# Value matmuls of an attention unit in two groups of eight instead of four groups of four

## What is computed

```python
att = jnp.einsum('bhqd,bhkd->bhqk', q, k) * scale
att = jnp.where(causal[None, None], att, -jnp.inf)      # self attention only
y = jnp.einsum('bhqk,bhkd->bhqd', jax.nn.softmax(att, axis=-1), v)
```

## Time and profile before

| what | value |
|---|---|
| median of three runs | 1836.56 us |
| the profiled execution: span from first to last instruction | 1831.7 us |
| TensorE busy | 1634.0 us, 89% |
| VectorE busy | 1353.5 us, 74% |
| ScalarE busy | 1151.3 us, 63% |
| GpSimd busy | 658.3 us, 36% |
| mean granted TensorE clock | 0.957 of full |

### The profile page before, as it was taken

One profiled execution on the slowest core, in us unless ns is written; L12 is line 12 of the kernel. 1 busy time (PEld: TensorE's weight loads), 2 busy tenths in 40 slices (PEclk: granted clock), 3 DMA queues, 4 the chain that ended last, 5 costly groups with the idle time before them and its releaser, 6 DMA issues.

```text
span 1831.7 us, 29160 instructions
## 1 busy us (share of the span) xinstructions
PE 1634.0 (89%) x10051; PEld 735.1 (40%) x10064; DVE 1353.5 (74%) x2549; ACT 1151.3 (63%) x2178; POOL 658.3 (36%) x915
## 2 busy tenths in 40 slices
PE   5897879998999989998999999988999998899677
PEld 1343335433543435433543344433543543333236
DVE  6677677788588777778687777877488687688287
ACT  1474576566755686667765685657655854756497
POOL 3422524550445234641454135622562242310140
PEclk7898989999999999999999999999999998899899
DMA  7333412323243323332242323332332231124123
GB/s 196 101 108 108 121 35 72 99 79 90 63 117 79 93 59 99 88 101 67 67 113 62 91 77 92 86 102 76 82 105 59 54 102 47 44 77 138 46 70 116
DMA packets 106947, 159.49 MB, mean 87 GB/s; under 512 B 20656, under 2 KB 83248, under 8 KB 106800
## 3 DMA queue, kind: packets, MB, share of 16 engines
q1 hardware_dynamic: 101904, 156.43, 30.8%
q10 hardware_dynamic: 4896, 1.18, 0.3%
HBM read 105.00 MB, written 51.38 MB: 85 GB/s over the span
## 4 chain that ended last, share of the span: by engine, by line
PE 54%; DVE 19%; ACT 10%; POOL 7%; issue 4%; DMA 3%; SPq 1%; ACTq 0%; DVEq 0%; POOLq 0%
PE acc L1492 11%; PE st L1478 10%; PE misc L1457 10%; DVE nmax L1255 8%; PE misc L1432 7%; PE misc L1404 4%; PE misc L1519 3%; PE misc L1444 3%; ACT probs L988 3%; ACT tail_h L1058 2%; ACT tail_h L1043 1%; PE misc L1546 1%; PE misc L1533 1%; POOL parts L873 1%; POOL qk L869 1%
## 5 line engine op out<-in xcount | busy, mean ns | idle before, releaser
L1255 DVE TENSOR_REDUCE nmax<-misc 128x1 f32<-128x512 f32 (+2 forms) x1376 | 863.8, 671 | 301.9 <-PE misc L1457 181.4
L988 ACT ACTIVATE probs<-st 128x512 f32<-128x512 f32 (+3 forms) x1536 | 760.4, 551 | 375.2 <-PE st L1478 241.3
L1457 PE MATMUL misc<-stack 96*128 96x512 bf16 (+3 forms) x1536 | 535.1, 364 | 58.2 <-DVE nmax L1255 41.1
L1478 PE MATMUL st<-stack 99*128 99x512 bf16 (+3 forms) x1536 | 539.8, 362 | 37.6 <-ACT probs L988 31.5
L1478 PEld LDWEIGHTS st<-stack 99*128 99x128 bf16 x1536 | 148.7, 98 | 377.8 <-ACT probs L988 222.0
L1457 PEld LDWEIGHTS misc<-stack 96*128 96x128 bf16 x1536 | 151.9, 99 | 199.1 <-DVE nmax L1255 83.1
L1492 PE MATMUL acc<-probs,v_x 128*32 128x512 f32 x1152 | 157.8, 621 | 0.0
L867 POOL TENSOR_TENSOR parts<-qk,zero 128x512 bf16<-128x512 f32 x78 | 81.3, 1043 | 207.6 <-ACT qk L971 207.6
L879 POOL TENSOR_TENSOR nparts<-nmax,zero 128x16 bf16<-128x16 f32 x96 | 21.3, 222 | 273.3 <-DVE nmax L1255 273.3
L1492 PE MATMUL acc<-probs,v_s 128*32 128x512 f32 (+3 forms) x1152 | 113.6, 466 | 0.1
L1481 PE MATMUL st<-mask_st,identb 128*128 128x128 bf16 x512 | 111.1, 220 | 0.0
(11 more groups left out here) (258 smaller groups left out, 2087.2 us busy)
## 6 DMA issues: line engine op xcount, KB each, us to landing
parts_xk<-parts SPq DMA_DIRECT2D x54, 128.0 KB
parts_xq<-parts SPq DMA_DIRECT2D x54, 128.0 KB
stack<-parts_xq SPq DMA_DIRECT2D x36, 192.0 KB, 3.2
stack<-parts_xk SPq DMA_DIRECT2D x36, 192.0 KB, 3.7
parts_sk<-parts SPq DMA_DIRECT2D x48, 128.0 KB
parts_sq<-parts SPq DMA_DIRECT2D x48, 128.0 KB
stack<-parts_sq SPq DMA_DIRECT2D x32, 192.0 KB, 2.9
stack<-parts_sk SPq DMA_DIRECT2D x32, 192.0 KB, 3.4
```

Of the source, the lines that this page charges most:

```text
L988: act.activation(probs[:, j % P_SLOTS, c, T - w:], st_bank(n, 4 * j + c)[:, 0:w], ACT.Exp, scale=SCALE).then_inc(exp_done, 1)
L1255: dve.tensor_reduce(nmax[:, ring, first:first + NT * (len(cs) - 1) + 1:NT], src, AX.X, ALU.max, negate=True).then_inc(misc_free[slot], 1)
L1457: last = pe.matmul(o, stack[0:ROWS, r, 0, c, P * i:P * i + P], stack[0:ROWS, r, 1, c, 0:w], start=True, stop=not causal)
L1478: last = pe.matmul(o[:, 0:w], stack[0:AUG, r, 1, c, P * j:P * j + P], stack[0:AUG, r, 0, c, T - w:T], start=True, stop=not causal)
```

## The change

The four value groups of a unit become two, each for two tile rows (a pair, `PAIRS` = 2): the first stands after the scores (2, 3), the second after the scores (0, 3) of the next unit. `probs` has three slots, taken in turn over all tile rows of all units, and the first exponential of a tile row waits for the pair that holds the tile row three before it. `v_aug` keeps 18 columns a head (`V_STEP`), of which the matmul takes 17 (`VW`); the zeros go, with the three memsets on GpSimd that made them, and VectorE clears `acc` once at the start, since the matmuls now write 17 of every 32 partitions and the heads copy reads all. The code that is not in this core of the diff only adjusts counts (`NMADE`, `AHEAD`, `VD`).

```diff
-ST_BANKS, MISC_BANKS, P_SLOTS, QK_RING = 3, 4, 2, 4
+ST_BANKS, MISC_BANKS, P_SLOTS, QK_RING = 3, 4, 3, 4
+PAIRS = NT // 2
+VW, V_STEP = D + 1, D + 2
...
-            if c == 3 and j:
-                out.append(("values", u, j - 1))
+            if (j, c) == (2, 3):
+                out.append(("values", u, 0))
             if (j, c) == (0, 3) and prev:
-                out += [("values", prev, NT - 1), ("heads_copy", prev)]
+                out += [("values", prev, PAIRS - 1), ("heads_copy", prev)]
...
-    return [("values", u, NT - 1), ("heads_copy", u), ("heads_out", u)]
+    return [("values", u, PAIRS - 1), ("heads_copy", u), ("heads_out", u)]
...
-        v_aug = {p: lb(f"v_{p}", [P, NT, H, 32]) for p in "xsf"}
+        v_aug = {p: lb(f"v_{p}", [P, NT, H, V_STEP]) for p in "xsf"}
...
+        def probs_slot(n, j):
+
+            tile_ = n.times(NT, j).base
+            return tile_ % P_SLOTS, max(0, (tile_ - P_SLOTS) // 2 + 1)
...
                 pool.memset(v[:, :, :, D:D + 1], 1.0).then_inc(consts_made, 1)
-                pool.memset(v[:, :, :, D + 1:], 0.0).then_inc(consts_made, 1)
...
-                if c == 0:
-                    act.wait_ge(values_done, n.times(4, VD - P_SLOTS + j + 1).at())
+                slot, freed = probs_slot(n, j)
+                if c == 0 and freed:
+                    act.wait_ge(values_done, freed)
                 act.wait_ge(st_full, n.times(16, 4 * j + c + 1).at())
-                act.activation(probs[:, j % P_SLOTS, c, T - w:], st_bank(n, 4 * j + c)[:, 0:w], ACT.Exp, scale=SCALE).then_inc(exp_done, 1)
+                act.activation(probs[:, slot, c, T - w:], st_bank(n, 4 * j + c)[:, 0:w], ACT.Exp, scale=SCALE).then_inc(exp_done, 1)
...
             dve.memset(stack[ROWS:AUG, :, 1, :, :].bitcast(F32), two_ones).then_inc(ones_made, 1)
+            dve.memset(acc[:, :], 0.0).then_inc(ones_made, 1)
...
-                j, n, (_, p, g) = s.args[0], s.n, s.unit
-                w = T - P * j if p == "s" else T
-                if j == 0:
+                pair, n, (_, p, g) = s.args[0], s.n, s.unit
+                if pair == 0:
                     pe.wait_ge(v_done[p], s.b.times(2, 2).at())
                     pe.wait_ge(heads_full, n.at(1))
-                pe.wait_ge(exp_done, n.times(16, 4 * j + 4 + ST_BANKS).at())
-                for c in range(HU):
-                    last = pe.matmul(acc[32 * c:32 * c + 32, T - w:T], v_of(s, p)[:, j, HU * g + c, :],
-                                     probs[:, j % P_SLOTS, c, T - w:T], start=j == 0, stop=j == NT - 1)
+                pe.wait_ge(exp_done, n.times(16, 8 * pair + 8 + ST_BANKS).at())
+                for j in (2 * pair, 2 * pair + 1):
+                    w = T - P * j if p == "s" else T
+                    slot, _ = probs_slot(n, j)
+                    for c in range(HU):
+                        last = pe.matmul(acc[32 * c:32 * c + VW, T - w:T], v_of(s, p)[:, j, HU * g + c, 0:VW],
+                                         probs[:, slot, c, T - w:T], start=j == 0, stop=j == NT - 1)
                 last.then_inc(values_done, 1)
```

More of the change, by code:

```diff
@@ L496, in two_layers_kernel @@
         NFIRST = 6
-        NMADE = 13
+        NMADE = 10
         consts_in, consts_made = sem("consts_in"), sem("consts_made")
@@ L525, in two_layers_kernel @@
         zeroed, waited, picked = sem("zeroed"), sem("waited"), sem("picked")
-        AHEAD = [(free, 1) for free in misc_free] + [(exp_done, ST_BANKS), (values_done, P_SLOTS), (heads_full, 1), (negmax_split, 8), (negmax_landed[0], 16),
+        AHEAD = [(free, 1) for free in misc_free] + [(exp_done, ST_BANKS), (heads_full, 1), (negmax_split, 8), (negmax_landed[0], 16),
                  (negmax_landed[1], 16),
                  (y_summed, 1), (stored, 32)] + [(p, 48) for p in parts_out] + [(q, 4) for q in qk_split]
-        VD = P_SLOTS
         SCALARS = 15
@@ L984, in scores @@
                 w = T - P * j if s.unit[1] == "s" else T
-                if c == 0:
-                    act.wait_ge(values_done, n.times(4, VD - P_SLOTS + j + 1).at())
+                slot, freed = probs_slot(n, j)
+                if c == 0 and freed:
+                    act.wait_ge(values_done, freed)
                 act.wait_ge(st_full, n.times(16, 4 * j + c + 1).at())
-                act.activation(probs[:, j % P_SLOTS, c, T - w:], st_bank(n, 4 * j + c)[:, 0:w], ACT.Exp, scale=SCALE).then_inc(exp_done, 1)
+                act.activation(probs[:, slot, c, T - w:], st_bank(n, 4 * j + c)[:, 0:w], ACT.Exp, scale=SCALE).then_inc(exp_done, 1)
             def heads_copy(s):
-                act.wait_ge(values_done, s.n.times(4, VD + 4).at())
+                act.wait_ge(values_done, s.n.times(PAIRS, PAIRS).at())
                 if s.n.base or s.i is not None:
@@ L1360, in consts_rest @@
                 pe.wait_ge(consts_in, 16 * (NCONST - NFIRST))
-                pe.wait_ge(ones_made, 1)
+                pe.wait_ge(ones_made, 2)
             def weights(s):
```

## The result

The kernel after takes 1868.41 us (median of four runs) against 1839.07 us for the kernel before on the same chip: a ratio of 1.0153, 95% interval 1.0125 to 1.0181. One of its four runs took 2621.26 us, at a mean granted clock of 0.554, and is not in the ratio; the others took 1861.08, 1862.65 and 1874.18 us. It is 1.5% slower, some 28 us; the forecast was 1819, 1% faster, and the range ended at 1834.

A forecast was written before the change was run, and what follows sets the result against it. TensorE was taken to bound most of the kernel, nine units of twelve; 36.5 - 9.1 - 5 - 4 - 0.5 - 0.9 = 17 us gained, from 1836.56 to 1819 us, range 1800 to 1834.

The forecast's parts named there:

- What a group costs, and the gross gain: On TensorE a value group occupies 1.09 us; each of 192 merges saves 0.19 us, 36.5 us gross.
- the rival of exposed loads: Each join of two groups exposes a weight load: 15 us gross, 1 to 6 us gained, 1833; chance 0.07.
- (b): Runs of eight scores and maxima between groups overrun banks: 0.07 us in half of 144 merges, 5 us lost, at most 22.
- Buffers eat it: Score and shared banks, sized for runs of four, cost 0.14 us a run, 20 us in all: 1835; chance 0.13.
- (a): In three units of twelve, paced by VectorE or ScalarE, the saving buys nothing: minus a quarter, 9 us.
- (c): Where ScalarE paces, it may idle 0.9 us longer a group: 29 us at worst, 4 us taken.
- the slower rival: ScalarE starves at 0.9 us a group in the units it paces: 1844 to 1859, taken at 1846; chance 0.09.
- Columns, slots and v writes: 17 columns for 32, three probability slots and v writes with a step of 18: 0 us taken for each.
- 0.9 forecast: The heads copy waits 0.9 us longer for its group, but nothing moves from the group's end to the heads' transposes.
- the 0.5: At the start, clearing the accumulator on VectorE ahead of the first statistics adds about 0.5 us to the path.
- the signs named for being wrong: 17-column passes of another length, exponential waits grown over 4 us a turn, or a granted clock falling where it was full.
- the 0.9 us taken there: At the kernel's end, all of the last joined group waits for the last exponentials: 0.9 us lost.

The follow-up runs named there:

- moved_fours: Against `slots_fours`, only the first group moved from behind scores (1,3) to behind (2,2), nothing merged: 1865.54 us, 1.0166 of the kernel before.
- slots_fours: The kernel before with 17 of 18 columns a head and three probability slots, four groups at their old places: 1835.08 us, 0.9975.
- last_pair: The kernel after with only the last two groups merged, the first two separate at their old places: 1826.75 us, 0.9938 of the kernel before.
- first_pair: The kernel after with only the first two groups merged, behind scores (2,3), the other two separate: 1871.87 us, 1.0186 of the kernel before.
- the light kernels: Maxima and exponentials over a quarter of the columns: narrow groups of four 1739.69 us, the kernel after 1740.97 us, the latter with two steps moved 1730.49 us.

## Why the prediction was wrong

**What a group costs, and the gross gain: right, a little low.** 47 us for 36.5, some 5 of them from the narrower columns, for which the prediction took 0. No load is exposed at the join, as the two rows 0.44 and 0.43 us after the first show, so the rival of exposed loads is out. With it goes, for these loads, the rule of the Trainium skill that the prediction had weighed ("TensorE: Matmul & The Clock Gate", Part 3, The mechanism): loads in the same row groups do run under the passes here.

**(b), longer runs without a value group: the step that failed.** It took 5 us, at most 22. `moved_fours` measures what the longer run in front of the first group costs without any merge: 30 us, for a run of seven, to which the working gave nothing. The working looked only at the run's own scores and maxima, and held that "with projections between, which give both engines time, nothing" is lost. But other steps stand in that run which themselves wait for others: the transposes of the split maxima and of the attention sum. The group that was taken away had been the work that hid their waits. Of the 28 us lost, 17 came back when GpSimd's splitting and the step of the attention sum were moved. In `moved_fours` the wait for the split maxima, 13.7 us more than before, is less than half of the 30; most of the rest goes with the clock, which stood at its lower level up to 24 us of work time longer between (2,0) and (3,0). That split is a sum from the traces: no run held the clock.

**The banks.** The waits for VectorE and ScalarE grew by 7 and 8 us over the whole execution, and the new row at (2,3) adds 7 more; they did not go away with the two moves. "Buffers eat it" was thus a true second part: it bears on why the joins give so little, not on the 30 us, which `moved_fours` loses without it. All of TensorE's waits together are 180 us in `slots_fours`, 197 in `last_pair`, 200 in `moved_fours` and 216 in `first_pair`: each join brings some 17 us of waiting for the some 21 us that it saves. Why it does, and so the remaining 11 us over the kernel before, stays open; the light kernels leave it so even with short evacuations.

**(a) right.** Paced units stayed within 0.5 us, and give nothing.

**(c) and the slower rival: wrong.** ScalarE does not starve. What it waits for scores in a turn, before and after, in the view of the earlier trace rows:

```profile
ACT probs L988 <- PE st L1478: 23.9, 27, 3.1
```

```profile
ACT probs L994 <- PE st L1485: 22.0, 21, 3.1
```

And the unit that ScalarE paces went from 17.20 to 17.00. The slower side came by a mechanism that no rival named.

**The rest.** Columns, slots and v writes: nothing, as said. The heads copy waits (81.5 - 23.9) / 96 = 0.60 us longer for its group, for 0.9 forecast; `last_pair` has the same (83.0 us in all) and does not lose. At the start, the clearing of 0.48 us and the later first statistics on GpSimd (8.15 for 7.56) bear out the 0.5:

```profile
5.23 0.48 DVE L1071 MEMSET acc<- 128x512 f32 x1
...
8.15 0.24 POOL L833 TENSOR_SCALAR rstd_A<-mv_A 128x4 f32<-128x4 f32 x1 [3.64 <-DVE mv_A L1161]
```

Of the signs named for being wrong, the last one came: a granted clock that falls where it was full. At the end the heads copy starts 2.03 us after the last exponential instead of 1.19, so the 0.9 us taken there came as 0.84.

The parts add up roughly: 1835.1 (`slots_fours`) + 30.5 for the move, + 6.3 for joining the moved groups (`first_pair` less `moved_fours`), - 8.3 for the last join (`last_pair`) makes 1863.6; measured 1861.08 to 1874.18. The two joins thus give 2 us together, of some 42 (the first with the move from (2,2) to (2,3) in it).

## What to carry to other kernels

When work is moved in an engine's queue, price what it covered where it stood: list the steps behind its old place that wait for another engine, and by how little they were in time. Merging is safest at a place where one of the groups already stands; here the last join, made there, gave 8 us and the first, which had to move, lost. A small hole costs more than its length when the clock falls behind it, as it did here.

## What the runs showed of the hardware

Two fp32 groups on the same four column tiles join without a seam: passes 0.43 us apart throughout, while changing between such a group and a full-array product costs 0.09 us going in and about 0.12 coming out (1.84 less four passes of 0.43). Groups with stationary operands of 17 and of 32 columns take nearly the same time, 0.985 and 0.998 us up to the next score.

At half the granted clock, in the stretch at 0.50 above, the work went at about half its pace: the maxima matmul started 0.42 us after its score (775.70 to 776.12) instead of 0.22. The eight transposes, which ran into that stretch, took 1.56 us instead of 1.09, and the joined group, which ran out of it, 2.65 instead of 1.91. In the 4.4 us ahead of these transposes TensorE was busy 3.27 us, where it had been busy 3.99 before; half a microsecond after they began the clock fell, and it stayed at 1.2 GHz for 3.4 us, where it had stayed full before.
